# Edge slots under counting and ranking, and a state-space loop whose every fourth slot has none

## What is computed

```
xn    = layer_norm(x)
# graph attention, 4 heads of 64
proj  = xn @ gat_w.T;  e = leaky_relu(s_src[src] + s_tgt[dst])
agg   = segment_sum(proj[src] * softmax_over_target(e), dst)
# state-space model over the nodes, in the order of their degree
deg   = segment_sum(1, src);  perm = argsort(deg + noise);  inv = argsort(perm)
y     = mamba(xn[perm])[inv]      # 16 states: h = exp(dt*A)*h + (dt*x)*B;  y = h @ C
# both joined by a gate, a feed-forward layer, and 8 experts with 2 per node
out   = x + gate(norm(elu(agg + xn)), norm(xn + y)) ... + experts(...)
```

## Time and profile before

| | us |
|---|---|
| median of three runs | 4287.28 |
| profiled execution | 4285.63 |
| its span, first to last instruction | 4284.0 |
| PE, DVE busy | 3021.3, 3010.5 |
| POOL, ACT busy | 2331.1, 1979.5 |
| mean granted PE clock, share of full speed | 0.839 |

### The profile page before, as it was taken

How to read it: one execution, slowest core, us unless ns; L and a number is a source line. 1 busy time by engine, 2 the same in 40 slices (tenths; PEclk the granted TensorE clock), 3 DMA queues, 4 the chain that set the end, 5 groups by cost and what they waited for, 6 DMA issues and landing times. The chain is left out here.

```text
span 4284.0 us, 66432 instructions
## 1 busy us (share of the span) xinstructions
PE 3021.3 (71%) x17205; PEld 2270.9 (53%) x17206; DVE 3010.5 (70%) x5576; ACT 1979.5 (46%) x4255; POOL 2331.1 (54%) x2215
## 2 busy tenths in 40 slices
PE   5333321177887888778887788787877488939998
PEld 4333311155655565556655565555655245528887
DVE  6677795478788878888788888888887488721111
ACT  2000000066666656666666666666665265613222
POOL 2000003557777777777777777777775357633443
PEclk8555555589998999999999999999998799969999
DMA  3100201334444444445444444444447433326665
GB/s 100 34 0 0 100 1 41 106 96 132 125 124 128 131 127 125 130 129 133 125 126 130 129 128 129 125 127 132 126 128 103 115 73 96 89 95 144 142 144 108
DMA packets 282877, 457.71 MB, mean 107 GB/s; under 512 B 56232, under 2 KB 202905, under 8 KB 282265
## 3 DMA queue, kind: packets, MB, share of 16 engines
q0 software_dynamic: 119472, 287.74, 28.4%
q1 hardware_dynamic: 163048, 165.86, 13.1%
HBM read 389.97 MB, written 63.43 MB: 106 GB/s over the span
## 5 line engine op out<-in xcount | busy, mean ns | idle before, releaser
L679 POOL DMA_INDIRECT el_g<-table,el_ix x1792 | 1796.5, 1003 | 689.7 <-issue 520.6
L1094 PE MATMUL fl_ps<-el_g,el_oh 128*128 128x260 f32 x3584 | 1029.4, 438 | 336.0 <-DVE ACC L802 333.0
L1094 PEld LDWEIGHTS fl_ps<-el_g,el_oh 128*128 128x128 f32 x3584 | 747.6, 215 | 707.5 <-issue 554.5
L822 DVE TENSOR_TENSOR_SCAN mb_h<-mb_dA,mb_h,mb_dB 128x224 f32<-128x224 f32 x896 | 573.9, 672 | 0.0
L792 DVE TENSOR_TENSOR el_g<-el_g,fl_pw 128x1024 f32<-128x1024 f32 x448 | 544.2, 1215 | 0.0
L953 ACT CAST el_oh<-fl_pt 128x512 f32<-128x512 bf16 x451 | 261.0, 579 | 425.0 <-PE fl_pt L1070 421.7
L1117 PE MATMUL fl_py<-mb_hc,ident 128*128 128x448 f32 x896 | 422.2, 553 | 0.1
L968 ACT ACTIVATE mb_dA<-mb_dt,mb_a 128x224 f32<-128x224 f32 x900 | 382.6, 475 | 2.9 <-DVE mb_dt L866 1.6
L811 DVE TENSOR_TENSOR mb_dB<-mb_u,fl_pbc 128x448 f32<-128x448 f32 x449 | 276.3, 615 | 135.4 <-PE fl_pbc L1107 134.5
L468 POOL DMA_INDIRECT sorted_x<-XN,rank x49 | 47.8, 975 | 588.8 <-DVEq L388 574.2
L939 ACT ACTIVATE el_away<-el_dst,el_less 128x512 bf16<-128x512 bf16 x452 | 325.3, 720 | 22.1 <-DVE mb_a L756 21.2
(11 more groups left out here) (300 smaller groups left out, 5405.8 us busy)
## 6 DMA issues: line engine op xcount, KB each, us to landing
el_dst<-dst_rows SPq DMA_DIRECT2D x452, 128.0 KB
el_g<-table,el_ix POOLq DMA_INDIRECT x1792
ex_w<-in_moe_W SPq DMA_DIRECT2D x56, 512.0 KB
ex_x<-routed_x SPq DMA_DIRECT2D x56, 257.0 KB, 2.8
mb_x<-sorted_x SPq DMA_DIRECT2D x30, 224.0 KB, 3.2
table<-px_tr POOLq DMA_DIRECT2D x49, 130.0 KB, 2.3
px_x<-in_x SPq DMA_DIRECT2D x49, 128.0 KB, 2.6
xn<-XN SPq DMA_DIRECT2D x1, 6272.0 KB
```

What stands on the lines that cost most here:

```text
L679: pool.indirect_dma_start(out=G[b // GU][:, b % GU * NJ + j, :], out_offset=None, in_=dram["table"], in_offset=bass.IndirectOffsetOnAxis(a ...
L822: nc.vector.tensor_tensor_scan(H[:, n % 2, k, :], dA[:, n % 4, k, :], dB[:, n % 2, k, :], H0[:, k, n % NS:n % NS + 1], ALU.mult, ALU.add). ...
L1094: mm = nc.tensor.matmul(pS, OH[:, n % (2 * GU), j, :], G[n // GU % 2][:, n % GU * NJ + j, :], start=j == 0, stop=j == NJ - 1)
```

## The change

`degrees`, `ranks` and the resident tile XN are gone as stages. `project` stores xn to DRAM from POOL's queue, tile by tile, out of XS; it no longer writes XN. `pair_tables` follows it at once. `streams` takes the place of `both_loops` and has three blocks on all engines, with a barrier between them:

1. 36 edge slots; in 34 of them one chunk of the count with DB = 46 columns. The layout is now [value, column]: both inputs and the output of a comparison have the columns innermost, the values come from a tile REP in which each value is repeated 46 times, and TensorE reads its operands with a step of 46 elements. The wait on the count matmuls is for the chunk before the last one in every slot.
2. 56 edge slots; in 49 of them one tile of the ranking, small and large tiles by turns.
3. The weights, 4 edge slots in which POOL also scatters the 49 tiles (brought back from DRAM by SP into nine buffers), 8 edge slots in which the 16 steps of preparation of chunk 0 are done in pairs, and the loop: 448 state slots, 24 edge slots per body of 32. Slots 0, 4, 8 and 12 of 16 have no edge work.

There are 104 + 14 x 24 = 440 edge slots in all, where there were 448. The gathers run 5 slots ahead over a barrier (G_LEAD). The logits' group of four now starts in slots 1, 6 and 11 of a chunk.

```diff
-DB = 34
+DB = 46
+ND = DC // DB
 NS, DR, CONV = 16, 16, 4
 TC, RB = 224, 112
 TS = TC // RB
 NC = NP // TC
 SLOTS = NC * NS
 BODY = 32
+GB = 24
+G_COUNT, G_RANK, G_INTRO, G_LEAD = 36, 92, 104, 5
+PAIRS = G_INTRO + NC // 2 * GB
...
+def pair(q):
+    return Slot(0, q, GB)
+def pair_beside(m):
+    at = m.n % 4 - 1
+    return Slot(m.i, G_INTRO + m.n // 4 * 3 + at, GB) if at >= 0 else None
...
-                    at = w["XN"][:, bass.ds(i * TG + j, 1), :].rearrange("p o d -> p (o d)")
-                    nc.vector.tensor_scalar(at, X[:, j, :], MV[:, j, 0:1], RS[:, j:j + 1],
-                                            ALU.subtract, ALU.mult)
                     dve.wait_ge(turned, 1 + i * TG)
+                    dve.wait_ge(kept_xn[j], 16 + i * 16)
...
+            from_sixteen(pool, w, dram, *kept_xn)
             with pool.Fori(0, NT // TG) as i:
+                for j in range(TG):
+                    pool.wait_ge(scaled, 1 + i * TG + j + 1)
+                    pool.dma_start(n_t[bass.ds(i, 1), j, :, :].rearrange("o p d -> p (o d)"), XS[:, j, :]
+                                   ).then_inc(kept_xn[j], 16)
...
+        def free(pool, p):
+            if not early(p.number, 2 * GU):
+                pool.wait_ge(s["summed"], p.number - 2 * GU + 1)
+                apart(pool, s["passed"])
...
+        def edges_vector(dve, S):
+            steps = logits(dve, S) if S.n % GU == 0 else None
+            if steps:
+                next(steps)
+                next(steps)
+                next(steps)
+            add(dve, S - 3)
+            if steps:
+                next(steps)
+                next(steps)
+            scale(dve, S - 1)
+        def edges_scalar(act, S):
+            one_hot(act, S + GU)
+            keep_turned(act, S + (GU - 1))
+            if S.n % GU == 0:
+                weights(act, S)
+                weights_again(act, S)
+        def edges_tensor(pe, S):
+            turn(pe, S + (GU - 1))
+            spread(pe, S + (GU - 1))
+            if not early(S.number, 2):
+                gather_sums(pe, S - 2)
...
+        HA, HB = sb("dg_ha", [P, 2, SRC_HI, DB], BF16), sb("dg_hb", [P, 2, SRC_LO, DB], BF16)
...
+        for q in range(G_COUNT + G_LEAD):
+            free(pool, pair(q))
+            gather(pool, pair(q), srcT[:, q, :])
...
+        def mark_high(c):
+            if c >= 2:
+                dve.wait_ge(counted, c - 1)
+            nc.vector.tensor_tensor(HA[:, c % 2], HI[:, c * DB:(c + 1) * DB].unsqueeze(1).to_broadcast([P, SRC_HI, DB]),
+                                    REP[:], ALU.is_equal).then_inc(split_hot, 1)
+        def mark_low(c):
+            nc.vector.tensor_tensor(HB[:, c % 2], LO[:, c * DB:(c + 1) * DB].unsqueeze(1).to_broadcast([P, SRC_LO, DB]),
+                                    REP[:, 0:SRC_LO, :], ALU.is_equal).then_inc(split_hot, 1)
+        for q in range(G_COUNT):
+            S = pair(q)
+            steps = logits(dve, S) if q % GU == 0 else None
+            if steps:
+                next(steps)
+            if q < ND:
+                mark_high(q)
+            if steps:
+                next(steps)
+                next(steps)
+            if q >= 3:
+                add(dve, S - 3)
+            if steps:
+                next(steps)
+                next(steps)
+            if q >= 1:
+                scale(dve, S - 1)
+            if q < ND:
+                mark_low(q)
+        dve.wait_ge(counted, ND)
+        nc.vector.tensor_tensor(key[:], count[:], noise[:], ALU.add).then_inc(keyed, 1)
...
+        for q in range(G_COUNT):
+            edges_tensor(pe, pair(q))
+            c = q - 1
+            if 0 <= c < ND:
+                pe.wait_ge(split_hot, 2 * c + 2)
+                for e in range(DB):
+                    mm = nc.tensor.matmul(count[:], HA[:, c % 2, :, e], HB[:, c % 2, :, e], start=c == 0 and e == 0,
+                                          stop=c == ND - 1 and e == DB - 1, skip_group_check=True)
+                mm.then_inc(counted, 1)
...
+    tile_at = [t for u in range(NT // 2) for t in (u, NT - 1 - u)] + [NT // 2]
+    first = G_COUNT + 5
...
+        for q in range(G_COUNT, G_RANK):
+            if q == first:
+                dve.wait_ge(loaded, 32)
+                dve.wait_ge(turned_k, 1)
+                done(nc.vector.tensor_copy(KC[:], pK[:]))
+            edges_vector(dve, pair(q))
+            if first <= q < first + NT:
+                compare(q - first)
...
+    XN = [t[:].rearrange("p b k t -> p (b k t)")[:, u * D:(u + 1) * D] for t in (dB, H, HC) for u in range(3)]
...
+    SCAT, PREP = 4, 8
...
+        each = -(-NT // SCAT)
+        for k in range(SCAT + PREP):
+            p = pair(G_RANK + G_LEAD + k)
+            free(pool, p)
+            gather(pool, p, srcT[:, p.number, :])
+            for t in range(k * each, min((k + 1) * each, NT)):
+                b = t % len(XN)
+                pool.wait_ge(xn_loaded[b], t // len(XN) * 16 + 16)
+                pool.indirect_dma_start(
+                    out=dram["sorted_x"], in_=XN[b], in_offset=None,
+                    out_offset=bass.IndirectOffsetOnAxis(ap=w["rank"][:, t:t + 1], axis=0)).then_inc(placed[b], 16)
...
+        ahead, each = len(XN), -(-NT // SCAT)
+        for t in range(ahead):
+            bring(t)
+        for k in range(SCAT):
+            for t in range(ahead + k * each, min(ahead + (k + 1) * each, NT)):
+                bring(t)
+            rows(sp, pair(G_RANK + k + 4))
+        for b in range(len(XN)):
+            sp.wait_ge(placed[b], -(-(NT - b) // len(XN)) * 16)
+        load(0)
+        for k in range(SCAT, SCAT + PREP):
+            rows(sp, pair(G_RANK + k + 4))
+        load(1)
...
+        def slot(M, S):
+            n, c = M.n, M.of(NS)
+            at, b = n % NS, n // NS % 2
+            if at == 1 and not early(c, 1):
+                give_out(c - 1, 1 - b)
+            if not early(M.number, 1):
+                read_out(M - 1)
+            steps = logits(dve, S) if S and S.n % GU == 0 else None
+            if steps:
+                next(steps)
+            scan(M, 0)
+            if steps:
+                next(steps)
+            scan(M, 1)
+            if steps:
+                next(steps)
+            if S:
+                add(dve, S - 3)
+            if steps:
+                next(steps)
+                next(steps)
+            if S:
+                scale(dve, S - 1)
+            prepare(c + 1, 1 - b, at)
+            inflow(M + 1)
...
+        for k in range(SCAT):
+            edges_vector(dve, pair(G_RANK + k))
+        for k in range(PREP):
+            edges_vector(dve, pair(G_RANK + SCAT + k))
+            for at in range(k * NS // PREP, (k + 1) * NS // PREP):
+                prepare(0, 0, at)
+        inflow(Slot(0, 0))
+        run(dve, slot)
...
+            if S:
+                turn(pe, S + (GU - 1))
+                spread(pe, S + (GU - 1))
+            copies(M + 1)
+            if not early(M.number, 1):
+                sum_up(M - 1)
+            if S:
+                gather_sums(pe, S - 2)
```

More of the change, by code:

```diff
@@ new lines, in free, with gather @@
+        def free(pool, p):
+            if not early(p.number, 2 * GU):
+                pool.wait_ge(s["summed"], p.number - 2 * GU + 1)
+                apart(pool, s["passed"])
+        def gather(pool, p, index):
+            b = p.n % (2 * GU)
+            for j in range(NJ):
+                pool.indirect_dma_start(
+                    out=G[b // GU][:, b % GU * NJ + j, :], out_offset=None, in_=dram["table"],
+                    in_offset=bass.IndirectOffsetOnAxis(ap=index[:, j:j + 1], axis=0)).then_inc(gathered[b], 16)
@@ new lines, in one_hot @@
+        def one_hot(act, p):
+            q, n = p.number, p.n
+            act.wait_ge(brought[n % 4], p.of(4) * 16 + 16)
+            if not early(q, 1):
+                act.wait_ge(s["hot"], q)
+            nc.scalar.activation(AWAY[:], DST[:, n % 4, :], ACT.Abs, bias=LESS[:, 0:1]).then_inc(s["away"], 1)
+            if not early(q, 2):
+                act.wait_ge(s["turned"], q - 1)
+                act.wait_ge(s["spread"], q - 1)
+            act.wait_ge(s["away"], q + 1)
+            nc.scalar.activation(OHT[:, n % 2, :], AWAY[:], ACT.Relu, bias=1.0, scale=-1.0).then_inc(s["hot"], 1)
@@ new lines, in keep_turned, with weights, weights_again @@
+        def keep_turned(act, p):
+            q, n = p.number, p.n
+            act.wait_ge(s["turned"], q + 1)
+            if not early(q, 2 * GU):
+                act.wait_ge(s["summed"], q - 2 * GU + 1)
+            nc.scalar.copy(OH[:, n % (2 * GU)], pT).then_inc(s["turned_sb"], 1)
+        def weights(act, p):
+            act.wait_ge(s["shifted"], p.of(GU) + 1)
+            nc.scalar.activation(G[p.n // GU % 2][:, :, D:], DM[:], ACT.Exp)
+        def weights_again(act, p):
+            if not early(p.number, 1):
+                act.wait_ge(s["scaled"], p.number)
+            nc.scalar.activation(weight, DM[:], ACT.Exp).then_inc(s["weight"], 1)
```

(31 more changed lines are left out.)

1223 lines of the change are left out of this document (573 added, 650 removed).

## The result

The changed kernel takes 4300.68 us (median of 8 runs, 4297.8 to 4309.62), the kernel before 4284.25 (8 runs). The ratio is 1.0039, its 95% interval 1.0026 to 1.0051: slower by 0.4%, where 4016 us was forecast. The profiled execution has a span of 4305.2 us.

The account below looks back on a forecast made before the run. GpSimd's gathers were taken to hold the loop between convolutions, TensorE at them. 959.5 us ahead of the loop, 28 x 75 in it, 7 and 948 after, with 1.6 around, gave 4016 us, range 3890 to 4150.

Parts of the forecast that it names:

- the count operands: Counting: TensorE reading its operands with 92 bytes between elements was priced at zero, with slower reads left to a rival.
- rival E: Counting: strided operands slow TensorE; decides above 16.2 us a slot or 209 ns a pair; at three times today's, 4376; 5%.
- The opening: Start of the counting: clearing ACC, casts, and 16 gathers at 1.25 us with their landing, 25 us.
- Five slots ahead of the ranks: Start of the ranking block: five slots held by gathers, 18 us, which hide the loading of keys.
- 49 ranking slots: Ranking: comparisons 190 us plus edge work 96, and 8 for short comparisons outlasted by cold gathered sums.
- The counting slot's circle: Counting: mark-high, add, gathered sums and 46 count matmuls in turn, 6.9 us at the upper clock, 10.7 lower; 8.3 taken.
- the doubled rate of the comparisons: Counting: VectorE's comparisons at two elements a cycle, 2.5 and 1.6 us in place of 4.9 and 3.2.
- GpSimd hidden in the ranking: Ranking: GpSimd needs 56 x 5.0 = 280 us, hidden within the block's 320 us.
- scatter and preparation: Third block ahead of the loop: 49 scatters, 12 edge slots and the preparation chain, 147 us with a barrier.
- the loop: 448 state slots: 75 us a chunk in place of 87.7, VectorE work 65.9 and waits 9.0; 356 us saved.
- rival D: Loop: TensorE's convolution and logits right behind it keep the chunk at 81 us, +168, 4184; 12%.
- The wait "near 4 us" behind the convolution: Loop: sign that VectorE waits near 4 us a chunk on the copies of B and C; 3.8 in the sum.

Follow-up runs that it names:

- the layout experiment: Changed kernel with both count tiles laid out in pairs of columns, TensorE's step 4 bytes in place of 92: 4112.61 us, ratio 0.9592.
- the one series: Layout in pairs of columns alone in the kernel before, and three edits without and with rows ahead: 0.9725, 0.9505, 0.9526 against the kernel before at 4752.58 us.

## Why the prediction was wrong, and where it was right

**The step that failed** is the one on the count operands: "The count operands are now read with 92 bytes between elements [...] I take zero, as with the clock in the middle some of it is paid". It measured 183 ns a pair where 89 had been taken, and by the layout experiment it is some 190 of the 285 us by which the median missed. Nor did a low clock pay for it: the prediction's own 46 pairs at the lower clock are 4.1 us, and they took 8.43. The mechanism was written down as rival E with 5%, its only ground that no row showed such a price. That is no evidence against a price. A cost with no row in the trace and only one possible sign should have been bounded by more than its rival's threshold.

**Rival E's threshold** was 209 ns a pair, a slot of 16.2 us; measured 15.0. 183 is below it, and yet the kernel is slower: the threshold took all other terms as exact. The slots' own loss is 34 x 6.7 = 228 us, and the table's 290.7 leaves 63 for the other terms.

- **The opening** (25, measured 39.2): the clearing of ACC was in the sum, but not that it would hold the gathers, although showed VectorE holding one.
- **Five slots ahead of the ranks** (18, measured 34.6): they were said to be held by gathers, with the loading of the keys hidden; the target rows behind the keys on SP's queue were not counted. Of VectorE's waits there 3.3 us are on gathers, 8.4 on the sums, and 7.0 on ScalarE's weights, which stand behind its 16.96 us of wait for target rows. Rows ahead of the keys gave 6 us back; the other 10 of the miss are not taken apart.
- **49 ranking slots** (286 and 8 for short comparisons, measured 322.2): VectorE is busy 281.66 / 49 = 5.7 us a slot, as forecast; the waits are 0.8 a slot, 40.5 us, where the 8 were put. Of these 18.0 us are on the spread scores, which had no term, and 9.6 on the sums.
- **The counting slot's circle** was right as a chain, as the add that was moved ahead shows, but not its size: 9.4 us with fast matmuls, at a granted clock of 0.71. The 8.3 was a choice between 6.9 and 10.7 that no row backed; 8.0 was reached only with the add first, at 0.80.

**Right** were: the doubled rate of the comparisons (2.5 and 1.7 us); GpSimd hidden in the ranking; scatter and preparation (147, measured 142.2); and the loop, with VectorE busy 1827.54 / 28 = 65.3 us a chunk where 65.9 was forecast. The prediction has two small slips, on which nothing hangs: its rates give 4.0 us less of comparisons a slot and not 3.9 (3.9 is what was measured), and in rival D TensorE has 60 us of work left by its own terms, not 58. The loop's waits, 1260 to 3140 us or 25 chunks:

```profile
DVE mb_dB L1020 <- PE fl_pbc L1258: 98.3, 49, 3.6
DVE el_s L516 <- PE fl_px L604: 64.9, 49, 2.0
```

That is 3.9 us a chunk on the copies of B and C, against 3.8, and 2.6 on the scores, against 2.4; no wait on gathers is among the longer ones. The wait "near 4 us" behind the convolution is there, 3.6 at most in the one slot.

**Open** is why the moving operand costs more at 92 than at 64 bytes, what made the one series slower in the loop, and what a version would give in which the gathers don't meet the comparisons.

## What to carry over

When a layout is turned for one engine, count what the other engine reads with the new step: here 34 x 3.9 = 132 us less of VectorE's comparisons were bought with slots of 15.0 us in place of 9.4, 34 x 5.6 = 190 us, and columns in twos gave the one without the other. Of what a forecast prices at nothing, ask what stands behind it on the same queue or port. And when a change does much at once, time its parts alone: here some 3% was to be had by a layout in the old order of work.

## What the hardware showed that was not expected

TensorE's load and matmul of 98 stationary bf16 values with 16 bytes or more from one to the next take 167 to 183 ns, 1.7 to 1.9 ns a value, and at 16 bytes the same at either clock. While such groups ran alone and back to back and TensorE was busy without a gap, the granted clock fell from 1.00 over 0.86 to 0.50, and in the changed kernel's counting it is 0.56 with TensorE busy 81% of the time, while it is 0.80 in the counting of the kernel with the add first, where it is busy 63%:

```profile
214.10:487.00 272.90, 172.34 (x2099) 155.20 (x2100) 202.43 (x199) 67.86 (x122) 231.07 (x138) 0.80 0.32 83
```

So being busy on slow operands did not keep the upper clock in these runs. And VectorE's comparisons hold gathers about as long as they last (2.4 to 2.7 us beside one of 2.50 us): with the slow comparisons of the old layout GpSimd was busy 291.5 us for 144 instructions in the counting, with the fast ones 197.8 for 145.
